# Long attention: one burst of weighted sums per batch instead of three, with the pair sums, the turned maxima and the row sums moved to fit

## What is computed

```python
scores = jnp.einsum('bhsr,bhlr->bhsl', q_r, k_r)
attn = jax.nn.softmax(scores, axis=-1)
ctx_c = jnp.einsum('bhsl,bld->bhsd', attn, kv_rope)
```

## Time and profile before

| what | value |
|---|---|
| three runs | 2503.88 us median, 2502.15 to 2504.88 |
| the profiled execution, its own time | 2501.11 us |
| its span | 2499.3 us, 32566 instructions |
| TensorE matmul | 2275.3 us busy, 91% |
| TensorE weight load | 1593.7 us |
| VectorE | 1568.0 us, 63% |
| ScalarE | 958.4 us, 38% |
| GpSimd | 802.9 us, 32% |
| mean granted TensorE clock | 0.922 of full speed |

### The profile page before, as it was taken

The page is one execution under the profiler, slowest core; times in us unless marked ns, Lnnn a source line. Parts: engine busy times, 40 slices in busy tenths (PEclk is TensorE's granted clock), DMA queues, the critical chain, the costliest instruction groups (busy, mean ns, idle before and its releaser), DMA issues. The chain is left out here.

```text
span 2499.3 us, 32566 instructions
## 1 busy us (share of the span) xinstructions
PE 2275.3 (91%) x10844; PEld 1593.7 (64%) x10844; DVE 1568.0 (63%) x2615; ACT 958.4 (38%) x1429; POOL 802.9 (32%) x462
## 2 busy tenths in 40 slices
PE   6675998999999995998999999898899999995998
PEld 4454997655666554664566655697456666665997
DVE  2765444377777756687777776412677777754444
ACT  2432443334444441212444445111344444423443
POOL 0420332024444440362445444011034444421332
PEclk7877999789999997897999999879799999997999
DMA  4562631353434303123433431186733434202332
GB/s 79 165 205 66 224 112 59 117 134 84 116 90 102 86 22 119 41 79 103 103 86 94 111 83 48 53 292 249 215 82 87 106 83 111 60 6 79 119 118 82
DMA packets 112495, 266.98 MB, mean 107 GB/s; under 512 B 27969, under 2 KB 64747, under 8 KB 108440
## 3 DMA queue, kind: packets, MB, share of 16 engines
q1 hardware_dynamic: 111704, 263.64, 38.2%
q0 software_dynamic: 672, 1.84, 0.2%
HBM read 218.85 MB, written 46.41 MB: 106 GB/s over the span
## 5 line engine op out<-in xcount | busy, mean ns | idle before, releaser
L1229 DVE TENSOR_REDUCE keep_top<-banks 128x1 f32<-128x500 f32 x945 | 615.7, 675 | 257.6 <-PE banks L1162 254.4
L1291 ACT ACTIVATE att_ex<-banks 125x896 f32<-125x896 f32 x576 | 525.8, 918 | 259.6 <-PE banks L1151 237.5
L1341 POOL TENSOR_TENSOR att_acc<-att_acc,att_two 125x896 f32<-125x896 f32 x186 | 393.2, 2114 | 450.2 <-DVE att_two L1244 436.6
L1179 PE MATMUL banks<-att_ex,att_v 125*64 125x448 f32 x2304 | 464.7, 545 | 0.0
L1162 PE MATMUL banks<-keep_kh,keep_qt 128*128 128x500 f32 x945 | 349.8, 417 | 2.6 <-DVE keep_top L1229 2.2
L1244 DVE TENSOR_TENSOR att_two<-att_ex 125x896 f32<-125x896 f32 x288 | 313.5, 1127 | 49.3 <-ACT att_ex L1291 48.8
L1151 PE MATMUL banks<-keep_qt,keep_kh 128*125 128x448 f32 x1152 | 332.8, 370 | 2.3 <-ACT att_ex L1291 2.3
L1151 PE MATMUL banks<-att_qm,att_kl 65*125 65x448 f32 x1152 | 331.0, 368 | 0.0
L1179 PEld LDWEIGHTS banks<-att_ex,att_v 125*64 125x64 f32 x2304 | 152.5, 136 | 247.8 <-issue 200.3
L1619 PE MATMUL banks<-moe_xs,moe_w 128*128 128x448 f32 x1272 | 280.1, 370 | 23.8 <-DVE moe_xs L1734 23.0
L1619 PEld LDWEIGHTS banks<-moe_xs,moe_w 128*128 128x128 f32 x1272 | 242.9, 191 | 44.9 <-DVE moe_xs L1734 24.0
(11 more groups left out here) (244 smaller groups left out, 2379.5 us busy)
## 6 DMA issues: line engine op xcount, KB each, us to landing
keep_kh<-kvt_hi SPq DMA_DIRECT2D x96, 375.0 KB, 5.2
q_rows<-mats_q SPq DMA_DIRECT2D x24, 896.0 KB, 4.6
keep_qt<-q_rows SPq DMA_DIRECT2D x48, 448.0 KB, 6.2
moe_raw<-L_experts_dram SPq DMA_DIRECT2D x53, 384.0 KB, 4.1
att_kl<-kvt_lo SPq DMA_DIRECT2D x48, 375.0 KB, 7.9
att_v<-kvn SPq DMA_DIRECT2D x24, 720.0 KB
sort_wu<-L_experts_dram SPq DMA_DIRECT2D x14, 1024.0 KB, 10.6
moe_cb<-comb_rows SPq DMA_DIRECT2D x62, 224.0 KB
```

Source lines behind the costliest of these rows:

```text
L1179: last = pe.matmul(PS[WEIGHED][64 * e:64 * e + 64, 0:HALF], v[:, s // 2, u, s % 2, :], ex[:, u % RING, e, :], start=u == 0, stop=u == UNIT ...
L1229: dve.tensor_reduce(top[:, s % 2, n // NS, n % NS:n % NS + 1], PS[6 + (PIECES * s + n) % 2][:, 0:SB], AX.X, ALU.max).then_inc(mx_done, 1)
L1291: act.activation(ex[:, u % RING], scored, ACT.Exp).then_inc(exp_done, 1)
L1341: pool.tensor_tensor(a, two[:, 0] if n == 1 else a, two[:, n % 3], ALU.add).then_inc(gathered, 1)
```

## The change

`ex` gets 12 places, one per unit, and `two` goes. TensorE does all three rounds of scores and pieces first, then the turn of the maxima of b+1, then one burst of twelve units, and behind it the row sums of batch b-1 (in the last batch, where there is no turn, the row sums come ahead of the burst). VectorE does the six pairs behind all rounds; pair p is written into place p of `ex`, so it waits until unit p is weighed, and for the pair that last read the place. The reciprocals are of batch b-2 and come in round 1. ScalarE does twelve exponentials, `high`, the copy to `cu` and then the copy of the row sums of b-1; an exponential waits for the use of its place in the batch before. GpSimd places batch b-2 behind its second gather. SyncE does scales(b-2), shifts(b+1) and sums(b-1), in this order, behind the loads.

```diff
-RING = 4
+ROUND = 4
-        ex = st.sb("ex", [KP, RING, 2, HALF])
-        two, acc, one = st.sb("two", [KP, 3, 2, HALF]), st.sb("acc", [KP, 2, 2, HALF]), st.sb("one", [KP, 64])
+        ex = st.sb("ex", [KP, UNITS, 2, HALF])
+        acc, one = st.sb("acc", [KP, 2, 2, HALF]), st.sb("one", [KP, 64])
...
+                    if b >= 2:
+                        scales(b - 2)
+                    if b < B - 1:
+                        shifts(b + 1)
                     if b:
                         sums(b - 1)
-                        scales(b - 1)
-                    if b < B - 1:
-                        shifts(b + 1)
+                scales(B - 2)
...
-                    if not known(b, 2):
-                        pe.wait_ge(sm_done, b - 1)
+                    if not known(b, 3):
+                        pe.wait_ge(sm_done, b - 2)
...
+                def sums_of(a, b, turns):
+                    pe.wait_ge(gathered, GATHERS * b + GATHERS)
+                    pe.wait_ge(high_done, turns)
+                    sums([acc[:, a]])
...
-                        for u in range(4 * i, 4 * i + 4):
-                            weigh(s, b, u)
-                        if i == 0 and not known(b, 1):
-                            pe.wait_ge(gathered, GATHERS * b)
-                            pe.wait_ge(high_done, b + 1)
-                            sums([acc[:, (s + 1) % 2]])
-                        if i == 1 and left:
-                            turn((s + 1) % 4, b + 1)
+                    if left:
+                        turn((s + 1) % 4, b + 1)
+                    else:
+                        sums_of((s + 1) % 2, b - 1, b + 1)
+                    for u in range(UNITS):
+                        weigh(s, b, u)
+                    if left and not known(b, 1):
+                        sums_of((s + 1) % 2, b - 1, b + 2)
...
-                sums([acc[:, 1], two[:, 1], two[:, 2]])
+                sums([acc[:, 1], ex[:, PAIRS - 2], ex[:, PAIRS - 1]])
...
                     dve.wait_ge(exp_done, UNITS * b + 2 * p + 2)
-                    if p >= 3:
-                        dve.wait_ge(gathered, GATHERS * b + max(p - 3, 1))
-                    elif not known(b, 1):
-                        dve.wait_ge(gathered, GATHERS * b - GATHERS + p + 3)
-                    a = 2 * p % RING
-                    dve.tensor_tensor(two[:, p % 3], ex[:, a], ex[:, a + 1], ALU.add).then_inc(paired, 1)
+                    dve.wait_ge(pv_done, UNITS * b + p + 1)
+                    if p:
+                        dve.wait_ge(paired, PAIRS * b + p // 2 + 1)
+                    dve.tensor_tensor(ex[:, p], ex[:, 2 * p], ex[:, 2 * p + 1], ALU.add).then_inc(paired, 1)
...
-                        pair(b, 2 * i)
-                        pair(b, 2 * i + 1)
-                        if i == 1 and not known(b, 1):
-                            invert(s + 1, b - 1)
+                        if i == 1 and not known(b, 2):
+                            invert(s, b - 2)
+                    for p in range(PAIRS):
+                        pair(b, p)
+                    if not left:
+                        invert(s + 1, b - 1)
...
-                    if not (known(b, 1) and u < RING):
-                        act.wait_ge(pv_done, UNITS * b + u - RING + 1)
-                        act.wait_ge(paired, PAIRS * b + (u - RING) // 2 + 1)
+                    if not known(b, 1):
+                        act.wait_ge(pv_done, UNITS * (b - 1) + u + 1)
+                        if u < PAIRS:
+                            act.wait_ge(gathered, GATHERS * (b - 1) + max(u, 1))
+                        else:
+                            act.wait_ge(paired, PAIRS * (b - 1) + u // 2 + 1)
...
-                        if i == 0 and not known(b, 1):
-                            row_sums(b - 1)
-                        if i == 1 and left:
-                            high((s + 1) % 4, b + 1)
                     if left:
+                        high((s + 1) % 4, b + 1)
                         numerators(s, b)
+                    if not known(b, 1):
+                        row_sums(b - 1)
...
-                    pool.tensor_tensor(a, two[:, 0] if n == 1 else a, two[:, n % 3], ALU.add).then_inc(gathered, 1)
+                    pool.tensor_tensor(a, ex[:, 0] if n == 1 else a, ex[:, n], ALU.add).then_inc(gathered, 1)
...
-                        if n == 3 and b:
-                            place(b - 1)
+                        if n == 2 and b >= 2:
+                            place(b - 2)
+                place(B - 2)
```

More of the change, by code:

```diff
@@ L1179, in weigh @@
                         last = pe.matmul(PS[WEIGHED][64 * e:64 * e + 64, 0:HALF], v[:, s // 2, u, s % 2, :],
-                                         ex[:, u % RING, e, :], start=u == 0, stop=u == UNITS - 1)
+                                         ex[:, u, e, :], start=u == 0, stop=u == UNITS - 1)
                     last.then_inc(pv_done, 1)
@@ L1189, in sums @@
                     last.then_inc(sums_ready, 1)
+                def sums_of(a, b, turns):
+                    pe.wait_ge(gathered, GATHERS * b + GATHERS)
+                    pe.wait_ge(high_done, turns)
+                    sums([acc[:, a]])
                 def batch(s, b, left):
-                    for i in range(UNITS // 4):
-                        for slot in range(5):
+                    for i in range(UNITS // ROUND):
+                        for slot in range(ROUND + 1):
                             if slot:
-                                scores(s, b, 4 * i + slot - 1)
+                                scores(s, b, ROUND * i + slot - 1)
                             for ahead, n in pieces(i, slot, left):
                                 top_scores((s + ahead) % 4, b + ahead, n)
-                        for u in range(4 * i, 4 * i + 4):
-                            weigh(s, b, u)
-                        if i == 0 and not known(b, 1):
-                            pe.wait_ge(gathered, GATHERS * b)
-                            pe.wait_ge(high_done, b + 1)
-                            sums([acc[:, (s + 1) % 2]])
-                        if i == 1 and left:
-                            turn((s + 1) % 4, b + 1)
+                    if left:
[6 more added lines that the diff above has]
+                        sums_of((s + 1) % 2, b - 1, b + 2)
                 pe.wait_ge(qk_in[0], 48 + (l - 1) * B // 4 * 48)
@@ L1285, in exps @@
                     act.wait_ge(st_ready, UNITS * b + u + 1)
-                    if not (known(b, 1) and u < RING):
-                        act.wait_ge(pv_done, UNITS * b + u - RING + 1)
-                        act.wait_ge(paired, PAIRS * b + (u - RING) // 2 + 1)
+                    if not known(b, 1):
[4 more added lines that the diff above has]
+                            act.wait_ge(paired, PAIRS * (b - 1) + u // 2 + 1)
                     a = 2 * (u % 2)
                     scored = PS.all[0:KP, a * 512:a * 512 + 1024].rearrange("p (e k) -> p e k", e=2)[:, :, 0:HALF]
-                    act.activation(ex[:, u % RING], scored, ACT.Exp).then_inc(exp_done, 1)
+                    act.activation(ex[:, u], scored, ACT.Exp).then_inc(exp_done, 1)
                 def numerators(s, b):
@@ L1312, in batch @@
                 def batch(s, b, left):
-                    for i in range(UNITS // 4):
-                        for u in range(4 * i, 4 * i + 4):
+                    for i in range(UNITS // ROUND):
+                        for u in range(ROUND * i, ROUND * i + ROUND):
                             exps(b, u)
-                        if i == 0 and not known(b, 1):
-                            row_sums(b - 1)
-                        if i == 1 and left:
-                            high((s + 1) % 4, b + 1)
                     if left:
+                        high((s + 1) % 4, b + 1)
                         numerators(s, b)
+                    if not known(b, 1):
+                        row_sums(b - 1)
                 high(0, 0)
```

## The result

The changed kernel takes 2661.05 us (median of 4 runs, 2655.00 to 2666.41), the kernel before 2504.38 on the same chip: a ratio of 1.0625, interval 1.0611 to 1.0638. It is slower, by 157 us; the forecast of 2602 had 99, and its range ended at 2655. The profiled execution took 2655.0 with a span of 2653.2, 153.9 more than before.

What follows compares the result with a forecast made beforehand. TensorE's order was taken to set the pace. Per attention 11 x 1.7 + 1.2 + 1.1 + 8 = 29, three 87, loads 12: +99 on the profiled 2501.1 gives 2600, as a median 2602; range 2530 to 2655.

Steps and rivals of the forecast that it cites:

- Fewer bursts: On TensorE, two of three boundaries between pieces and bursts go: a gain of 0.7 us a batch.
- three pieces in a row: Where rounds join without a burst, TensorE's third piece waits for VectorE, 0.67 at each of two boundaries: 1.3 a batch lost.
- turn and way in 0.2: In TensorE's walk, the turn of the maxima and the step into the burst take 0.2 us together.
- Pairs and additions take turns: In the burst, VectorE's pairs and GpSimd's additions block each other whole; pairs end at 11.05, the burst at 9.15.
- The wait on `cu`: ScalarE's copy waits for the placing of b-2, starting 2.95 behind the burst; late exponentials cost TensorE 1.3 a batch.
- That 0.6 lies inside the 1.4: The pairs' overhang delays the next reduction by 0.6, hidden inside TensorE's 1.4 wait for the first exponential.
- Batches 0 to 2 have no place to wait for: +0.4 each: The first three batches of each attention have no wait on placing and lose only 0.4 each.
- The queue: Loads of b+2 stand behind the row sums' way out and land late: some 3, 3 and 6 us, 12 together.
- The last batch: At each attention's end, weighing starts after all units are scored and additions come behind it: +8.
- Batch 14: This batch of each attention has one boundary of pieces less but the late exponentials: +1.1.
- the 2655 case: Rival: loads set the pace, more landing at 8 to 8.8, another 1.5 in 36 batches; chance 0.08.

Runs made afterwards that it cites:

- experiment 7: Changed kernel with SyncE issuing keys and queries first, then the row sums of two batches ago, then the other loads: 2648.45.
- Experiment 5: Changed kernel with four places for `cu`, plus GpSimd's additions only after all six pairs and its placing last: 2605.72.
- Experiments 1 and 2: Two separate edits of the changed kernel: four places for `cu` instead of two, 2619.30; GpSimd's placing ahead of the burst's first addition, 2637.50.
- experiment 6: Changed kernel with 26 unread TensorE products behind each attention's last burst, ahead of the last row sums: 2661.67.
- experiment 9: Changed kernel with its one burst cut in three again, two pairs added per round, all else of the change kept: 2504.94.
- experiment 4: Changed kernel with the row sums' way out through memory moved behind all of the next batch's loads in SyncE's queue: 2715.29.

## Why the prediction was right and wrong

**Fewer bursts and three pieces in a row: right in kind, undersized. The first failed step.** The third piece starts 1.16 behind the first (727.16 to 728.32), forecast 1.13. But the walk from there to the next scores takes 1.49 (727.16 to 728.65; 875.58 to 877.07 the second time), and I had 1.36: a piece that restarts TensorE holds the following unit off for 0.33, not the 0.23 of the earlier trace rows. Scores that restart cost 0.1 in the same way (725.20 to 726.12, for 0.81). I had priced these from rows in which TensorE never stood still. The last piece, turn and way in take 0.63 (739.20 to 739.83), where I had 0.43. That is no restart: the turn takes 0.31 in the kernel before too, and my "turn and way in 0.2" left most of it out. TensorE's timeline before:

```profile
2080.54 0.39 PE L1169 MATMUL banks<-ident,keep_nm 128*7 128x128 f32 x2
2080.85 0.72 PE L1162 MATMUL banks<-keep_kh,keep_qt 128*128 128x500 f32 x2
```

Together 0.1 + 2 x 0.13 + 0.2 = 0.56 a batch: 28.0 for 27.45. Over 33 batches that is 18 us, and 5 more in the other batches. The 28.14 of experiment 7 against 28.0 is another 5 us, which stays open.

**Pairs and additions take turns: right.** Experiment 5 shows it with the same instructions in another order: 1.72 against 1.09 a pair. By the Trainium skill, SBUF — State Buffer, "Who interferes with whom", VectorE work with two inputs and GpSimd's reads exclude each other. The trace agrees.

**The wait on `cu`: right to 0.2.** The copy starts 3.2 behind the burst (3.4 in some batches) for 2.95. Experiments 1 and 2 show the chain, place to copy to exponential.

**"That 0.6 lies inside the 1.4": right only where there is a placing. The second failed step.** The pairs reach 2.1 to 2.4 behind the burst in every batch (1.9 in my walk). From the burst of batch 2 on the late exponentials hide most of it. Behind the bursts of batches 0 and 1 there is no placing to wait for, and the overhang stands bare. VectorE's last pair and reductions, and TensorE's piece, behind the burst of batch 0:

```profile
546.92 3.00 DVE L1250 TENSOR_TENSOR att_ex<-att_ex 125x896 f32<-125x896 f32 x1
549.84 1.93 DVE L1237 TENSOR_REDUCE keep_top<-banks 128x1 f32<-128x500 f32 x3
...
550.56 0.49 PE L1165 MATMUL banks<-keep_kh,keep_qt 128*128 128x500 f32 x1 [1.39 <-DVE keep_top L1237]
```

The piece was due at 549.01 and starts 1.55 late; behind the burst of batch 1 it is 0.8. The periods are 27.5 where I had 26.15. "Batches 0 to 2 have no place to wait for: +0.4 each" took away the wait and with it its cover, without pricing what the cover hid. These batches cost 12.7 us more than forecast, but not all of it is this step. With a restart each, the two late pieces make 7.6 in three attentions, and 2.6 go off again, since no row sums stand in the first period. Some 4 are the short handovers above. Some 3 are scores at the lower clock level: the first period of the first attention took 29.07 (granted clock 0.72 from 550 to 556), and the first scores of the second attention ran at it 1.3 us longer than before.

**The queue: right in total, its parts by luck.** Late loads cost 10 to 13 (experiment 7) where I had 12. But held against experiment 7 the three attentions lose 5.9, 1.6 and 2.1 by them, and I had 3, 3 and 6. In the first attention landings were a little later than in the earlier trace rows, in the third they were earlier (median 6.1 for 7.0). The query load L635 in the first attention, after:

```profile
DMA to landing us min/median/max: 5.7/6.3/9.7
```

The Trainium skill, SBUF — State Buffer, "The DMA setup-cost knee", would have made this term 0, with its estimate of 3.05 us for this load. The traces don't agree, for a load among others: no landing of it in the changed kernel took less than 4.0.

**The last batch: the third failed step.** I had +8, it took +12.2, +15.2 and +12.9. One part is the burst's start: 17.5, 20.8 and 18.4 behind the end of the burst before, for 16 in my walk. The row sums that the change puts ahead of this burst take 0.8 and were not in the walk. The scores stand 2.54, 2.93 and 2.55 for the first exponential, and from there to the burst the mean granted clock is 0.86, 0.58 and 0.74. In experiment 6 the same three waits were followed by 0.58, 0.86 and 0.58, and the burst came after 20.4, 17.9 and 20.4: the lower the mean clock, the later the burst. The other part is the last sums. They waited for an addition until 977.75, 14.5 after the burst's start, nearly as my walk said (14.2), but then took 4.6, 4.2 and 4.4 instead of 2.5 (experiment 6). Windows and timeline of the second attention's last batch:

```profile
1640.00:1650.00 10.00, 7.07 (x25) 5.53 (x22) 2.52 (x2) 4.43 (x6) 9.51 (x5) 0.71 0.02 3
1650.00:1660.00 10.00, 10.00 (x33) 7.87 (x32) 0.00 (x0) 6.75 (x8) 0.00 (x0) 0.60 0.06 23
```

```profile
1645.24 1.11 PE L1154 MATMUL banks<-keep_qt,keep_kh 128*125 128x448 f32 x2 [2.93 <-ACT att_ex L1302]
```

In all three last batches some of the scores run at the lower of the two clock levels. I carried TensorE's durations over at full clock into a stretch where my own walk had it stand for 5 us. 16 us over three attentions. Batch 14 took 2.0 more than before, not 1.1; half of that is the same handovers.

**Sum.** By the table the forecast lacked 13 in the first batches, 21 in the 33 periods, 3 in batch 14 and 16 in the last batches: 53. By cause, handovers priced too low make some 24, the last batch 16, the bare overhang 5, the lower clock level in the first batches 3, and the longer periods for which no cause is shown 5. The mechanism, its places and its order held; what failed is the size of its terms, most of all TensorE's handovers and the last batch's durations at full clock. No rival came true; the 2655 case had the right size for another reason (the loads cost 10 to 13, not 12 + 54).

## What to carry to other kernels

Work of a neighbour engine that is spread between bursts is hidden because it is spread: gathered into one burst, it meets itself (here pairs and additions, which take turns), outlasts the burst, and every buffer that it frees comes late. Price a wait that is put in with what its cover hid and with the restart behind it, and price separately the batches in which it does not occur. Before four repairs are made to a change, undo its one central part alone: experiment 9 alone shows that nothing else in it mattered.

## What I had not expected of the hardware

- Two small transfers issued behind the loads and 720 KB of values took 10.1 to come back instead of 1.45; behind the loads without values it was 5 to 6.5 (experiment 4).
- After a wait a 128x500 product holds off the next unit for 0.33 instead of 0.23.
- Short waits of TensorE were enough for the lower clock level, but not each time. In the second attention's last batch 2.93 idle was followed by a mean granted clock of 0.58 up to the burst, in experiment 6 the same wait by 0.86. 5.3 idle was followed by sums at 1.7 to 1.9 times their usual duration. With pieces between the scores, 1.39 idle at 550.56 was followed by 0.72 from 550 to 556, while the third attention's window, where no wait was longer than 1.4, stayed at 1.00.
